# Tables of a hand-ordered program drawn anew, parameters loaded first, and the angles of the S4D kernel's passes made by GpSimd in a stage of their own

## What is computed

```python
x = x + cross_attention(ln(x), ctx, mask)      # 8 heads of 64, 64 context tokens
x = x + routed_mlp(ln(x))                      # 16 experts of 64, sigmoid, best 4 of 16
x = x + text_block(ln(x), ctx)                 # attention over the best 32 keys, FiLM,
                                               # S4D convolution, FiLM, gelu ffn
x = x + expert_choice_ffn(ln(x))               # 8 experts, each takes the best 512 tokens
```

```python
dtA = exp(log_dt)[:, None] * (A_re + 1j * A_im)
dC = C * (exp(dtA) - 1.0) / A
K = 2.0 * einsum('dn,dnl->dl', dC, exp(dtA[:, :, None] * arange(L))).real
```

## Time and profile before

| | us |
| --- | --- |
| median of 3 runs | 1483.37 (1480.74 to 1483.84) |
| the profiled execution | 1478.11 |
| its span on the core | 1476.3 |
| PE busy, share of the span | 1273.9, 86% |
| DVE busy | 924.8, 63% |
| ACT busy | 465.7, 32% |
| POOL busy | 326.4, 22% |
| from one trip's scores transposes to the next (497.26 to 623.10) | 125.84 |

### The profile page before, as it was taken

How to read it: one execution, slowest core, us unless ns; L and a number is a source line. 1 busy time by engine, 2 the same in 40 slices (tenths; PEclk the granted TensorE clock), 3 DMA queues, 4 the chain that set the end, 5 groups by cost and what they waited for, 6 DMA issues and landing times. The chain is left out here.

```text
span 1476.3 us, 17460 instructions
## 1 busy us (share of the span) xinstructions
PE 1273.9 (86%) x5230; PEld 764.1 (52%) x5230; DVE 924.8 (63%) x3439; ACT 465.7 (32%) x837; POOL 326.4 (22%) x598
## 2 busy tenths in 40 slices
PE   2777968999899899899989988999797629999996
PEld 2444644555466455546546544555354516666764
DVE  6746798767767676876776776687976292221110
ACT  2634531143234315304332530432322333232221
POOL 3311220033022103202301320222203203342321
PEclk9977969999999999999999999999998858999999
DMA  9002002000300300120030012012000124453321
GB/s 287 15 15 58 18 1 70 3 18 15 87 18 1 102 18 1 38 65 18 2 101 18 2 30 72 16 32 57 7 1 1 40 106 162 95 150 96 87 24 18
DMA packets 44904, 72.51 MB, mean 49 GB/s; under 512 B 8101, under 2 KB 26760, under 8 KB 44682
## 3 DMA queue, kind: packets, MB, share of 16 engines
q1 hardware_dynamic: 38666, 62.87, 14.6%
q0 software_dynamic: 6144, 8.52, 3.2%
HBM read 58.27 MB, written 13.07 MB: 48 GB/s over the span
## 5 line engine op out<-in xcount | busy, mean ns | idle before, releaser
L749 POOL TENSOR_SCALAR ve<-mv 128x2 f32<-128x2 f32 x74 | 16.7, 225 | 592.5 <-DVE mv L1017 592.4
L1580 PE MATMUL ps<-x,keys 128*128 128x512 f32 x256 | 129.0, 628 | 2.7 <-DVE hT L1109 2.7
L1737 PE MATMUL ps<-hT,values 128*128 128x512 f32 x256 | 118.6, 593 | 0.0
L2165 PE MATMUL experts_ps<-experts_yT,experts_fc 128*128 128x512 f32 x256 | 113.4, 601 | 1.3 <-ACT experts_yT L2090 1.3
L2177 PE MATMUL experts_ps<-experts_fc,experts_hT 128*128 128x256 f32 x512 | 112.1, 380 | 0.8 <-ACT experts_hT L2102 0.8
L1580 PE MATMUL ps<-zT_second,w 128*128 128x512 f32 x224 | 104.2, 606 | 6.8 <-ACT big L1528 6.1
L2177 PEld LDWEIGHTS experts_ps<-experts_fc,experts_hT 128*128 128x128 f32 x512 | 96.7, 190 | 14.6 <-ACT experts_hT L2102 1.6
L2074 DVE SCALAR_TENSOR_TENSOR experts_o<-experts_ps,experts_wh,experts_b2w 128x256 f32<-128x256 f32 x32 | 15.5, 484 | 140.2 <-PE experts_ps L2177 140.2
L1580 PE MATMUL ps<-w,big 128*128 128x256 f32 x448 | 99.1, 380 | 1.6 <-ACT big L1528 1.6
L2102 ACT ACTIVATE experts_hT<-experts_ps,experts_b 128x512 f32<-128x512 f32 x64 | 44.0, 687 | 157.2 <-PE experts_ps L2165 157.2
L1580 PEld LDWEIGHTS ps<-w,big 128*128 128x128 f32 x448 | 84.2, 190 | 14.1 <-ACT big L1528 3.2
(11 more groups left out here) (436 smaller groups left out, 2470.7 us busy)
## 6 DMA issues: line engine op xcount, KB each, us to landing
gT<-expert_gates SPq DMA_DIRECT2D x16, 1024.0 KB, 10.6
experts_fc<-in_fc1T SPq DMA_DIRECT2D x8, 1024.0 KB, 5.7
experts_fc<-in_fc2T SPq DMA_DIRECT2D x8, 1024.0 KB, 9.4
xT<-in_xT SPq DMA_DIRECT2D x8, 512.0 KB, 3.6
x<-in_x SPq DMA_DIRECT2D x8, 512.0 KB, 3.5
expert_table<-tb SPq DMA_DIRECT2D x7, 528.0 KB, 10.3
out_x<-x SPq DMA_DIRECT2D x7, 512.0 KB, 9.5
w<-in_W SPq DMA_DIRECT2D x2, 1024.0 KB, 9.0
```

Source lines behind the costliest of these rows:

```text
L749: nc.gpsimd.tensor_scalar(o, i, c, None, ALU.add).then_inc(*tick(*event))
L1580: last = nc.tensor.matmul(o, l, r_, start=start, stop=stop)
L1737: last = nc.tensor.matmul(bank("O2", k), S["values"][:, c, k * P:(k + 1) * P], hT[:, c % RING, :], start=(c == 0), stop=(c == HC - 1))
L2165: last = nc.tensor.matmul(g_bank(m), fc1[e % 3][:, k, m * P:(m + 1) * P], yT[e % 2][:, k, :], start=(k == 0), stop=(k == DC - 1))
```

## The change

The tables: OPENING grows from 128 to 166 stages and now reaches into the first trip (up to `mlp.7` of batch 1), ORDER starts and ends at another point of the trip and is ordered anew inside too, trips 0 to 2 take it in place of 0 to 3, and CLOSING grows from 360 to 443 stages. Both kernels run every stage once per batch; only `angles` is new. Two more moves in the tables: `bias` from between attention's parts to behind `gates.2`, and `choose` from inside layer 7 to the table's end. `fold_film` goes from the attention of batch 0 to the picks of its text attention.

The code (the tables cut to a few of their lines):

```diff
 OPENING = [
-    (KERN, 0, "steps", 0), (KERN, 0, "steps", 1), (KERN, 0, "centre", 0), (KERN, 0, "means"), (ATTEND, 0, "keys", 0),
+    (KERN, 0, "steps", 0), (KERN, 0, "centre", 0), (KERN, 0, "steps", 1), (ATTEND, 0, "keys", 0), (KERN, 0, "means"),
+    (KERN, 0, "angles", 0), (KERN, 0, "centre", 1), (ATTEND, 0, "keys", 1), (KERN, 0, "phases", 0), (KERN, 0, "powers", 0),
...
+    (ATTEND, 2, "spread"), (MID, 2, "relu", 0), (MID, 2, "mlp", 0), (LAST, 1, "film", 0), (LAST, 0, "table"), (MID, 2, "mlp", 1),
...
+    (LAST, 6, "route_experts"), (LAST, 7, "scores", 0), (LAST, 7, "shift_scores"), (LAST, 7, "scores", 1), (LAST, 6, "table"),
+    (LAST, 7, "route_experts"), (LAST, 7, "table"), (LAST, 7, "choose"),
 ]
-FULL_FROM, FULL_TO = 0, 4
+FULL_FROM, FULL_TO = 0, 3
...
-    y.declare("exponents_made", [("k_ex", p) for p in passes])
+    y.declare("exponents_made", [(e, p) for p in passes for e in ("k_base", "k_ex")])
...
+            sp.dma_start(ldt, A["log_dt"].partition_broadcast(P)).then_inc(par_in, 16)
+            for dst, src in ((aim, A["A_imT"]), (are, A["A_reT"])):
+                for rows_ in (slice(0, NS), slice(NS, P)):
+                    sp.dma_start(dst[rows_, :], src).then_inc(par_in, 16)
             sp.dma_start(ctx0[:], ctx_h[0]).then_inc(*tick("ctx0_loaded"))
             load("wk", kv_in)
+            for dst, src in ((cre, A["C_reT"]), (cim, A["C_imT"])):
+                for rows_ in (slice(0, NS), slice(NS, P)):
+                    sp.dma_start(dst[rows_, :], src).then_inc(coef_in, 16)
+            sp.dma_start(dskip, A["D_skip"]).then_inc(coef_in, 16)
             load("wv", kv_in)
-            for rows_ in (slice(0, NS), slice(NS, P)):
-                for dst, src in ((are, A["A_reT"]), (aim, A["A_imT"]), (cre, A["C_reT"]), (cim, A["C_imT"])):
-                    sp.dma_start(dst[rows_, :], src).then_inc(par_in, 16)
-            sp.dma_start(ldt, A["log_dt"].partition_broadcast(P)).then_inc(par_in, 16)
...
-            sp.dma_start(dskip, A["D_skip"]).then_inc(skip_in, 16)
...
-            def phases(_, p):
+            def angles(_, p):
                 if p == 0:
                     g.wait_ge(*at(0, "k_coef"))
                 else:
                     g.wait_ge(*at(0, "k_ex", p - 1))
+                if p >= 2:
+                    g.wait_ge(*at(0, "k_taps", p - 2))
+                some = spin[:, p * PC:(p + 1) * PC].unsqueeze(2)
+                g.tensor_tensor(Us[p % 2], some.to_broadcast([P, PC, LI]), it_i[:].unsqueeze(1).to_broadcast([P, PC, LI]), ALU.mult)
+                g.tensor_tensor(WBs[p % 2], some.to_broadcast([P, PC, LJ]), it_j[:].unsqueeze(1).to_broadcast([P, PC, LJ]),
+                                ALU.mult).then_inc(*tick("k_base", p))
+
+            def phases(_, p):
+                g.wait_ge(*at(0, "k_base", p))
                 if p >= 2:
                     g.wait_ge(*at(0, "k_pow", p - 2))
...
                     step(nc.vector.reciprocal(den, den))
+                    v.wait_ge(coef_in, 16 * 5)
                     mul(g[0], cre, are)
...
-                if p >= 2:
-                    v.wait_ge(*at(0, "k_taps", p - 2))
-                step(nc.vector.tensor_tensor(Us[k], over(spin, p, LI), it_i[:].unsqueeze(1).to_broadcast([P, PC, LI]), ALU.mult))
+                v.wait_ge(*at(0, "k_base", p))
                 step(whole_less(Us[k], Us[k], offA[:], wide))
-                step(nc.vector.tensor_tensor(WBs[k], over(spin, p, LJ), it_j[:].unsqueeze(1).to_broadcast([P, PC, LJ]), ALU.mult))
                 whole_less(WAs[k], WBs[k], offA[:], narrow).then_inc(*tick("k_phase", p))
...
-                    v.wait_ge(skip_in, 16)
...
-                    a.wait_ge(par_in, 16 * 9)
+                    a.wait_ge(par_in, 16 * 5)
                     nc.scalar.activation(ldt, ldt, ACT.Exp).then_inc(*tick("k_dt"))
```

More of the change, by code:

```diff
@@ L131 @@
-    (ATTEND, 0, "spread"), (MID, 0, "mlp", 1), (ATTEND, 0, "gates", 3), (KERN, 0, "phases", 4), (KERN, 0, "film_row"),
-    (KERN, 0, "powers", 3), (MID, 0, "relu", 0), (KERN, 0, "centre", 5), (MID, 0, "relu", 1), (MID, 0, "mlp", 2), (KERN, 0, "phases", 5),
-    (MID, 0, "mlp", 3), (MID, 0, "relu", 2), (MID, 0, "mlp", 4), (KERN, 0, "powers", 4), (MID, 0, "relu", 3), (MID, 0, "text", 0),
-    (MID, 0, "relu", 4), (KERN, 0, "phases", 6), (MID, 0, "mlp", 5), (MID, 0, "text", 1), (MID, 0, "mlp", 6), (MID, 0, "relu", 5),
@@ L147 @@
-    (ATTEND, 1, "gates", 3), (KERN, 0, "kernel", 5), (ATTEND, 1, "spread"),
+    (KERN, 0, "steps", 0), (KERN, 0, "centre", 0), (KERN, 0, "steps", 1), (ATTEND, 0, "keys", 0), (KERN, 0, "means"),
+    (KERN, 0, "angles", 0), (KERN, 0, "centre", 1), (ATTEND, 0, "keys", 1), (KERN, 0, "phases", 0), (KERN, 0, "powers", 0),
+    (KERN, 0, "angles", 1), (KERN, 0, "phases", 1), (KERN, 0, "masks"), (KERN, 0, "angles", 2), (KERN, 0, "phases", 2),
+    (KERN, 0, "centre", 2), (ATTEND, 0, "attend", 0), (ATTEND, 0, "norm"), (ATTEND, 0, "soften", 0), (ATTEND, 0, "keys", 2),
@@ new lines @@
+    (ATTEND, 0, "gates", 2), (KERN, 0, "angles", 4), (KERN, 0, "bias"), (ATTEND, 0, "gates", 3), (ATTEND, 0, "spread"),
+    (KERN, 0, "phases", 4), (KERN, 0, "film_row"), (KERN, 0, "centre", 4), (MID, 0, "mlp", 1), (KERN, 0, "powers", 3),
+    (KERN, 0, "centre", 5), (MID, 0, "relu", 0), (KERN, 0, "angles", 5), (MID, 0, "relu", 1), (KERN, 0, "phases", 5), (MID, 0, "mlp", 2),
+    (MID, 0, "relu", 2), (MID, 0, "mlp", 3), (MID, 0, "relu", 3), (KERN, 0, "angles", 6), (MID, 0, "mlp", 4), (KERN, 0, "powers", 4),
@@ new lines @@
+    (ATTEND, 1, "attend_out"), (ATTEND, 1, "gates", 0), (KERN, 0, "kernel", 3), (ATTEND, 1, "route"), (ATTEND, 1, "turn_route"),
+    (LAST, 0, "film", 0), (ATTEND, 1, "gates", 1), (ATTEND, 1, "gates", 2), (ATTEND, 1, "gates", 3), (KERN, 0, "kernel", 4),
+    (ATTEND, 1, "spread"), (LAST, 0, "film_in", 0), (KERN, 0, "kernel", 5), (LAST, 0, "film_in", 1), (LAST, 0, "film", 1),
+    (MID, 1, "relu", 0), (MID, 1, "mlp", 0), (MID, 1, "relu", 1), (LAST, 0, "fold"), (MID, 1, "relu", 2), (LAST, 0, "turn"),
@@ L169 @@
-    (MID, 1, "pick", 3, 2), (ATTEND, 2, "route"), (ATTEND, 2, "turn_route"), (LAST, 0, "scores", 0), (LAST, 0, "scores", 1),
-    (ATTEND, 2, "gates", 0), (ATTEND, 2, "gates", 1), (ATTEND, 2, "gates", 2), (ATTEND, 2, "gates", 3), (MID, 1, "picked", 0),
-    (LAST, 0, "shift_scores"), (MID, 1, "text", 2), (LAST, 0, "route_experts"), (ATTEND, 2, "spread"), (MID, 1, "pick", 3, 3),
-    (MID, 1, "picked", 1), (LAST, 0, "table"),
+    (MID, 1, "mlp", 8), (MID, 1, "mlp", 9), (MID, 1, "mlp_out"), (LAST, 0, "turn_back"), (LAST, 0, "hold"), (ATTEND, 2, "keys", 0),
@@ new lines @@
+    (MID, 4, "pick", 3, 3), (ATTEND, 5, "gates", 2), (ATTEND, 5, "gates", 3), (MID, 4, "picked", 0), (LAST, 3, "shift_scores"),
+    (LAST, 3, "scores", 1), (MID, 4, "text", 2), (MID, 4, "picked", 1), (LAST, 4, "film_in", 0), (LAST, 3, "route_experts"),
+    (ATTEND, 5, "spread"), (LAST, 4, "film_in", 1), (MID, 5, "relu", 0), (MID, 5, "relu", 1), (MID, 5, "mlp", 0), (LAST, 4, "film", 0),
+    (LAST, 4, "fold"), (LAST, 3, "table"), (MID, 5, "mlp", 1), (LAST, 4, "film", 1), (MID, 5, "relu", 2), (LAST, 4, "transform"),
@@ new lines @@
+    (LAST, 4, "scores", 1), (MID, 5, "text", 2), (LAST, 4, "shift_scores"), (LAST, 4, "route_experts"), (MID, 5, "picked", 1),
+    (ATTEND, 6, "spread"), (MID, 6, "mlp", 0), (LAST, 5, "film_in", 0), (LAST, 5, "film_in", 1), (MID, 6, "relu", 0), (LAST, 5, "fold"),
+    (LAST, 5, "film", 0), (LAST, 4, "table"), (MID, 6, "relu", 1), (MID, 6, "mlp", 1), (LAST, 5, "turn"), (MID, 6, "relu", 2),
+    (LAST, 5, "film", 1), (LAST, 5, "transform"), (MID, 6, "text", 0), (MID, 6, "mlp", 2), (MID, 6, "relu", 3), (LAST, 5, "hold"),
```

220 lines of the change are left out of this document (114 added, 106 removed).

## The result

The changed kernel takes 1474.24 us (median of 10, 1472.92 to 1477.33), the kernel before 1482.76 (median of 10). The ratio is 0.9948, with a 95% interval from 0.9936 to 0.9960: about 8 us less, where 18.7 were forecast. The profiled execution took 1472.92 us, its span is 1471.1 (before 1476.3).

A forecast was written before the change was run, and what follows sets the result against it. PE was taken to bound the trips and DVE much of the opening. Terms of -7.5 opening, +0.5 `fold_film`, -12 borders, -1.3 and +1.6 tail sum to -18.7 us, forecasting 1465 us, range 1453 to 1480.

The forecast's parts named there:

- I cost the loads at nothing: Start: loading parameters first gains 5 us, lost on ACT behind the copy of `sel`; coefficients at 28.3, worth 0.
- I put the shift itself at 0: Eight S4D kernel passes: moving two angle products from DVE to GpSimd is worth 0, bounds -6 and +5 us.
- I take 7.5 us: Opening: the new order of keys and `bias` around PE's waits for `powers` saves 7.5 us, from 0 to 8.
- ahead of the gates' transposes, where PE was waiting anyway: Opening: `bias`, moved from ahead of the second `powers` into an existing PE wait, saves 4.4 us.
- what is gained stays: Later opening: DVE is the bound there, so the gain made earlier, taken as 7.5 us, is kept.
- I take 3.0 a border ... four make 12: Trip borders: mlp and film matmuls fill PE's 3.05 us wait for scores, saving 3.0 each, between 0 and 4.8.
- as unchanged: Middle of the trips: stages are reordered, but their waits stay the same, give or take 1 us a trip.
- Tail, +0.3: End of trips: moving `choose` saves 1.3 us; layer 6's table work ahead of layer 7's tanh on ACT costs 1.6.
- (a): Main case: both the opening and the borders gain as forecast, giving 1465 us; chance 0.55.
- (c): Rival: the opening gains nothing because GpSimd is late in the passes; borders do gain: 1472 us; chance 0.15.
- (d): Rival: slower, as GpSimd's doubled work blocks DVE (+9.7 us) and borders gain 0: 1489 us; chance 0.10.
- the 0.5 of `fold_film`: Opening: `fold_film` on GpSimd now stands beside DVE's full stretch, costing 0.5 us.

The follow-up runs named there:

- loads_only: The kernel before with only the parameter loads of the change (loaded first, in two lots), old tables, angles on DVE: 1482.62 us, 0.9964.
- copy_behind: The changed kernel with angles on DVE and ACT's copy of `sel` back behind the rest of `steps`: 0.9889 of the kernel before.
- old_tables: The changed kernel's loads and GpSimd angles, with all stages in the order of the kernel before: 1485.88 us, 1.0028.
- products_twice: The changed kernel with angles on DVE, but GpSimd makes its own two products of each pass twice: 1476.78 us, 0.9946.
- angles_dve_3: The changed kernel with all its tables but the angles on DVE, second run: 1463.82 us, 0.9876 (first run 0.9902).
- dve_old_opening: The changed kernel with angles on DVE and the old order in the opening: 1459.61 us, 0.9836; run again (`_3`) 0.9872.
- border_only: The kernel before with only `table` moved behind the next trip's first mlp and film stages, at four borders: 1478.76 us, 0.9968.
- rest_only_3: The kernel before (its loads, angles on DVE, opening order) with only the new order of all stages behind the opening: 0.9886.
- bias_late_3: dve_old_opening with `bias` alone moved from ahead of the second powers to ahead of `centre.4`, second run: 0.9927.

## Why the prediction was wrong

The sign and the range held; the size did not: 8 us in place of 18.7. Two steps failed, the angles and the opening's order, and the border's term was mis-sized; a tail better than forecast hid part of it. By its steps:

1. "I cost the loads at nothing": right in this kernel. The head start was lost on ACT as forecast (coefficients at 27.36). By themselves, with the old order of ACT, they are worth 5.3 us (loads_only). The copy of `sel` accounts for a part of that at most: with it put back (copy_behind) the coefficients come 5 us earlier and the first powers only 2.5, since the keys' work on ACT stands in the way next, and the time can't be told from that of angles_dve.
2. "I put the shift itself at 0": this step failed, and it is the largest. The changed kernel with the angles on DVE is 7 to 11 us faster (0.9902 and 0.9876 to 0.9948); with the old opening it is 13 to 19 us (0.9836 and 0.9872 to 0.9961), and with the old order throughout 9.5 (old_tables and loads_only). My bounds were -6 and +5. They rested on three passes in which PE waits, and the trace before has two more (2.47 us at 109.58 and 4.74 at 197.18), but that is too little to explain it. I had counted the serial chain, with DVE's instructions at their time without GpSimd (0.75 and 1.23), and taken contention for a remark beside it. The trace after has 8.9 us of it in DVE's own pairs, and products_twice shows that it costs as much with no angle to wait for.
3. "I take 7.5 us" for the opening's order: failed. Its worth is 0 with the angles on DVE (0.9876 and 0.9872). Of its parts, the keys' early place makes the first powers 2.8 us later, since ACT's part of the stages moved too. `bias` stands "ahead of the gates' transposes, where PE was waiting anyway": it gave its 4.2 us to the second powers, but the same order puts `turn_route` behind the third, DVE waits 3.75 us for it, and 1.9 reach the transposes. I had looked at what moved out of PE's way and not at what moved into DVE's. That further on DVE is the bound and "what is gained stays" was wrong as well: `relu.0` is 2.1 us earlier and the first transform 9.5 later. In angles_dve_3 too the stretch between the two is longer than in dve_old_opening_3 (132.0 and 121.8 us), so this is the new order of the opening's second half, which I had not looked at, and not only GpSimd. Which stage in it costs is open.
4. "I take 3.0 a border ... four make 12": mis-sized. The four together are 5 us, 1.2 a border, from both sides. That nothing else waits was wrong: I had looked at x and keys, the inputs of the mlp, and not at `am`, the input of the film matmuls that were to fill the time, which DVE makes after the gates. Nor does the clock's loss go: it moves behind the next wait, and in border_only it is larger there (3.42 and 3.46 for 1.98 and 1.88, 3.0 us in all) than it was (3.62 for 1.88, 1.7 us).
5. The middle of the trip "as unchanged": not shown either way. rest_only_3 is worth 17 us; 7.5 of them are the tail's and some 5 the border's, which leaves about 4 for the order within the trips. But this is what is left of three measured terms with intervals of 3 to 4 us on either side, so it can't be told from nothing.
6. Tail, +0.3: mis-sized, it is -5 to -7.5 (with all that is behind layer 5's transform). `choose` gave its 1.3 (2.29 to 0.95). That layer 6's table work would push layer 7's by 1.6 was wrong: ACT comes to layer 7's tanh at 1167.21, 0.4 us after PE has ended its scores (1166.78). What I had not counted is PE's wait for layer 6's scores (2.86 to 0.64), and that layer 7's ffn no longer stands behind layer 6's scores matmuls.

Added up, the measured terms are 7 to 11 for the angles, 0 for the order of the opening, -5 for the borders, -5 to -7.5 for the tail and perhaps -4 for the trips: -3 to -9.5, and the measured 8 lies in that. As rivals, (a) had the sum of both gains and (c) an opening without gain. The time came out near (c)'s 1472, but by luck: the borders gave under half of their 12, the tail paid the difference, and (d)'s mechanism, GpSimd against DVE, was there at 7 to 11 us. The terms are not quite a sum: the opening by the trace is 9.5 us longer, and in angles_dve_3, whose first transform is as late as 264.61, the five trips behind it took 621.5 us against 630.3 in dve_old_opening_3 with the same order. It is not the slower opening that makes them shorter: in rest_only_3, with the old opening and the first transform at 257.03, they took 619.9. Why the same five trips take anything from 619.9 to 635.7 us (bias_late_3) is open; the granted clock differs with them (last section). In (d)'s sum the 0.5 of `fold_film` is missing; with it the 1489 stays.

dve_old_opening, the change without its order of the opening and without its angles, is the fastest version: 0.9836 and 0.9872 in two jobs, some 11 to 17 us faster than the changed kernel. rest_only_3, which needs no new code, can't be told from it (0.9886 beside 0.9872 in one job).

## What to carry to other kernels

A stage that is moved into the wait of one engine has parts on the others; look at the queue of the engine that ends the wait, for it is the one without room. Work that is moved to GpSimd from a DVE that it runs beside has to be priced by what DVE's remaining instructions took in the same trace beside GpSimd and without it (here 2.50 and 0.75 us), times their number, before the saving is counted. When a wait is filled, list the inputs of every instruction that is to fill it.
